# Attention outputs on one core: the values are read where they were projected, and the copy made for each head is given up

## What is computed

```python
q = x @ Wq
kv = x @ Wkv
k, v = jnp.split(kv, 2, axis=-1)
q, k, v = (to_heads(q), to_heads(k), to_heads(v))
sim = jnp.einsum('bid,bjd->bij', q, k) * scale
sim = sim + _cope(q, sim, pos_emb)
attn = jax.nn.softmax(sim, axis=-1)
out = jnp.einsum('bij,bjd->bid', attn, v)
```

## Time and profile before

| | |
|---|---|
| median of 3 runs | 2291.75 us (2290.97 to 2293.32) |
| the profiled execution's own time | 2291.38 us |
| its span, first to last instruction | 2289.5 us |
| mean granted TensorE clock | 0.993 of full speed |
| busy: TensorE, its weight loads, VectorE, ScalarE, GpSimd | 97%, 63%, 71%, 77%, 17% of the span |

### The profile page before, as it was taken

How to read it: one execution, slowest core, us unless ns; L and a number is a source line. 1 busy time by engine, 2 the same in 40 slices (tenths; PEclk the granted TensorE clock), 3 DMA queues, 4 the chain that set the end, 5 groups by cost and what they waited for, 6 DMA issues and landing times. The chain is left out here.

```text
span 2289.5 us, 53196 instructions
## 1 busy us (share of the span) xinstructions
PE 2226.8 (97%) x14577; PEld 1446.7 (63%) x14577; DVE 1633.4 (71%) x4269; ACT 1762.5 (77%) x3723; POOL 389.3 (17%) x673
## 2 busy tenths in 40 slices
PE   7999999999999999999999999999999879999997
PEld 5666666666666666666666666666665547777775
DVE  5888888888888888888888888888888811223232
ACT  5888888888888888888888888888888843455453
POOL 1111111111111111111111111111111101121121
PEclk9999999999999999999999999999999989999998
DMA  2010101010101010101010101010101021010100
GB/s 74 24 40 25 39 24 40 23 39 23 39 25 41 23 40 24 40 23 40 23 39 23 39 23 39 23 40 23 33 14 57 15 67 35 30 39 30 39 30 7
DMA packets 109392, 75.44 MB, mean 33 GB/s; under 512 B 28077, under 2 KB 105070, under 8 KB 109294
## 3 DMA queue, kind: packets, MB, share of 16 engines
q1 hardware_dynamic: 109294, 73.95, 11.6%
HBM read 14.33 MB, written 2.10 MB: 7 GB/s over the span
## 5 line engine op out<-in xcount | busy, mean ns | idle before, releaser
L842 DVE TENSOR_REDUCE mx<-Sc 128x1 f32<-128x1024 f32 (+1 forms) x512 | 568.0, 1130 | 245.1 <-PE Sc L632 244.8
L483 ACT ACTIVATE probsT<-rings 128x512 f32<-128x512 f32 x1024 | 554.1, 594 | 194.6 <-PE rings L640 194.4
L640 PEld LDWEIGHTS rings<-ident,probs 128*128 128x128 f32 x4096 | 437.0, 141 | 304.4 <-issue 103.1
L507 ACT ACTIVATE probs<-Sc,nbias 128x1024 f32<-128x1024 f32 x512 | 566.9, 1112 | 27.9 <-DVE nbias L852 27.9
L640 PE MATMUL rings<-ident,probs 128*128 128x128 f32 x4096 | 566.6, 281 | 3.0 <-ACT probs L507 2.5
L632 PE MATMUL Sc<-qk,q_now 64*128 64x512 f32 x2048 | 531.3, 616 | 10.5 <-ACT probs L507 9.1
L654 PE MATMUL out<-probsT,V_now 128*64 128x256 f32 x4096 | 498.3, 385 | 0.0
L805 DVE COPY_PREDICATED z<-mask,z 128x224 f32<-128x224 int16 (+5 forms) x768 | 393.3, 512 | 11.1
L375 POOL TENSOR_TENSOR prod<-cut,z 128x350 f32<-128x350 f32 x128 | 120.7, 943 | 1466.8 <-DVE z L817 1466.8
L654 PEld LDWEIGHTS out<-probsT,V_now 128*64 128x64 f32 x4096 | 271.4, 136 | 153.6 <-issue 42.5
L632 PEld LDWEIGHTS Sc<-qk,q_now 64*128 64x128 f32 x2048 | 177.5, 186 | 115.9 <-issue 100.6
(11 more groups left out here) (128 smaller groups left out, 2256.8 us busy)
## 6 DMA issues: line engine op xcount, KB each, us to landing
q_now<-qk SPq DMA_DIRECT2D x256, 64.0 KB, 2.0
xv<-xT SPq DMA_DIRECT2D x113, 128.0 KB, 2.2
q_far<-qk SPq DMA_DIRECT2D x256, 32.0 KB, 1.8
V_now<-V SPq DMA_DIRECT2D x16, 512.0 KB, 3.0
at<-attn SPq DMA_DIRECT2D x16, 512.0 KB, 3.2
probs<-in_x_dram SPq DMA_DIRECT2D x4, 512.0 KB, 5.5
wqk<-in_L_attn_Wq_dram SPq DMA_DIRECT2D x32, 64.0 KB, 2.1
xin<-in_x_dram SPq DMA_DIRECT2D x16, 128.0 KB, 2.8
```

The lines of the kernel that those rows point to most:

```text
L483: nc.scalar.activation(probsT[:, u, 4 * s:4 * s + 4, :], ring[k % 2][:, :].rearrange("p (t q) -> p t q", q=P), ACT.Copy).then_inc(slot_out, 1)
L507: nc.scalar.activation(probs[:, u, cols], Sc[:, cols], ACT.Exp, bias=nbias[:, u:u + 1], accum_out=sums[:, u, half:half + 1]).then_inc(exp_ ...
L640: last = nc.tensor.transpose(ring[k % 2][:, j * P:(j + 1) * P], probs[:, u, (4 * s + j) * P:(4 * s + j + 1) * P], ident[:, :])
L842: nc.vector.tensor_reduce(mx[:, u, half:half + 1], Sc[:, cols], AX.X, ALU.max).then_inc(dve_unit, 1)
```

## The change

The tile `V_now`, the semaphore `v_in`, the function `load_values` and all its 16 DMAs are taken out. `outputs` gets an argument `keys`, the head whose values it needs, and reads slot `keys % 4` of `V`. Since `outputs(g - 1, ...)` is issued in step `g`, the first step of a head passes the head before. The heads are written out one by one in TensorE's program, so `keys` is a plain number everywhere and the addresses are fixed ones.

```diff
-        V_now = sb("V_now", [P, NT, C])
...
-        v_in = sem("v_in")
...
-            def load_values(g):
-
-                sp.dma_start(V_now[:, :, :], V[:, (g // PAIRS) % 4, :, :]).then_inc(v_in, 16)
-
             sp.wait_ge(slot_out, 8 + 2 * PAIRS)
-            load_values(0)
...
                 load_now(g + 1, not odd)
-                if head:
-
-                    wait_apart(sp, out_full, g, waited)
-                    load_values(g)
                 if tile:
...
-            def outputs(g, base, slots, tiles, empty=True):
+            def outputs(g, base, slots, tiles, keys, empty=True):
 
                 if tiles[0] == 0:
                     if empty:
                         pe.wait_ge(halves_out, g)
-                    wait_apart(pe, v_in, g // PAIRS * 16 + 16, waited)
                 for t in tiles:
                     if t % 4 == 0:
                         pe.wait_ge(slot_out, base + slots[t // 4] + 1)
                     half = t % 2 * C
-                    last = nc.tensor.matmul(out[half:half + C, 0:2 * P], V_now[:, token_tile(t), :],
+                    last = nc.tensor.matmul(out[half:half + C, 0:2 * P], V[:, keys % 4, token_tile(t), :],
                                             probsT[:, :, t, :], start=t < 2, stop=t >= NT - 2)
...
             def head(at, par, start=0, **kw):
 
+                keys = at // PAIRS
                 if start == 0:
-                    body(at, False, par, new_keys=True, **kw)
-                    body(at + 1, True, par, **kw)
+                    body(at, False, par, new_keys=True, keys=keys - 1, **kw)
+                    body(at + 1, True, par, keys=keys, **kw)
```

More of the change, by code:

```diff
@@ L286, in _, with body @@
             weights(1)
-            def load_values(g):
-                sp.dma_start(V_now[:, :, :], V[:, (g // PAIRS) % 4, :, :]).then_inc(v_in, 16)
             sp.wait_ge(slot_out, 8 + 2 * PAIRS)
-            load_values(0)
-            def body(g, odd, late=False, first=False, tile=True, far=True, head=False, near=False):
+            def body(g, odd, late=False, first=False, tile=True, far=True, near=False):
                 base = slots_before(g, late)
@@ L323, in _ @@
             with sp.Fori(1, LASTV // PAIRS - 1) as h:
-                body(h * PAIRS, False, head=True)
+                body(h * PAIRS, False)
                 body(h * PAIRS + 1, True, near=True)
@@ L330, in _ @@
                 weights(h + 2)
-            body(LASTV - PAIRS, False, head=True)
+            body(LASTV - PAIRS, False)
             body(LASTV - PAIRS + 1, True, near=True)
@@ L336, in _ @@
             weights(H - 1, values=False)
-            body(LASTV, False, tile=False, head=True)
+            body(LASTV, False, tile=False)
             body(LASTV + 1, True, tile=False, near=True)
@@ L343, in _ @@
             load_early(sp, A, A["ctx_in"])
-            body(LASTP, False, late=True, tile=False, head=True)
+            body(LASTP, False, late=True, tile=False)
             body(LASTP + 1, True, late=True, tile=False)
@@ L667, in body @@
             def body(g, odd, par, late=False, first=False, proj=True, val=True, far=True, far_par=None,
-                     second=False, new_keys=False):
+                     second=False, new_keys=False, keys=0):
                 base = slots_before(g, late)
@@ L690, in body @@
                     transposes(1, base, at.last, 3)
-                    outputs(g - 1, base, at.last, range(EARLY_TILES), empty=not second)
+                    outputs(g - 1, base, at.last, range(EARLY_TILES), keys, empty=not second)
                 if far:
@@ L703, in body @@
                 if not first:
-                    outputs(g - 1, base, at.last, range(EARLY_TILES, NT))
+                    outputs(g - 1, base, at.last, range(EARLY_TILES, NT), keys)
                 if proj:
@@ L711, in head @@
             def head(at, par, start=0, **kw):
+                keys = at // PAIRS
                 if start == 0:
-                    body(at, False, par, new_keys=True, **kw)
-                    body(at + 1, True, par, **kw)
+                    body(at, False, par, new_keys=True, keys=keys - 1, **kw)
+                    body(at + 1, True, par, keys=keys, **kw)
                 with pe.Fori(2, PAIRS - 2, 2) as t:
-                    body(at + t, False, par, **kw)
-                    body(at + t + 1, True, par, **kw)
+                    body(at + t, False, par, keys=keys, **kw)
+                    body(at + t + 1, True, par, keys=keys, **kw)
                 if "late" in kw:
                     return
-                body(at + PAIRS - 2, False, par, far_par=1 - par, **kw)
-                body(at + PAIRS - 1, True, par, far_par=1 - par, **kw)
+                body(at + PAIRS - 2, False, par, far_par=1 - par, keys=keys, **kw)
+                body(at + PAIRS - 1, True, par, far_par=1 - par, keys=keys, **kw)
             body(0, False, 0, first=True)
@@ L730, in _ @@
             head(LASTP, 1, late=True, proj=False, val=False)
-            body(G - 2, False, 1, late=True, proj=False, val=False, far=False)
-            body(G - 1, True, 1, late=True, proj=False, val=False, far=False)
+            body(G - 2, False, 1, keys=H - 1, late=True, proj=False, val=False, far=False)
+            body(G - 1, True, 1, keys=H - 1, late=True, proj=False, val=False, far=False)
             base, at = slots_before(G, True), Slots()
@@ L741, in _ @@
             transposes(1, base, at.last, 3)
-            outputs(G - 1, base, at.last, range(NT))
+            outputs(G - 1, base, at.last, range(NT), H - 1)
             pe.wait_ge(scaled, 2 * (G - 1))
```

## The result

The changed kernel takes 2297.3 us (median of 10 executions, 2296.35 to 2301.3), the kernel before 2292.53 us (10 executions, 2290.66 to 2295.89). The ratio is 1.0024, 95% interval [1.0015, 1.0034]: 4.8 us slower, just over the 0.2% that the prediction called no change. The forecast was 2291.4 us and no change. The profiled execution of the changed kernel took 2296.35 us, with a span of 2294.3 us.

What follows compares the result with a forecast made beforehand. TensorE's own matmul stream was taken to bound the kernel. Terms 0 (wait) + 0 (tile) + 0 (15 copies) - 0.4 us (first copy) gave 2291.4 us, called no change, range 2288.5 to 2294.0 us.

Steps and rivals of the forecast that it cites:

- The wait ahead of the output matmuls, 128 times: TensorE's wait for copied values before each step's first output matmuls; removing it was put at 0 us.
- The tile: Output matmuls load weights from `V` instead of `V_now`; claimed cost 0, with 17 ns per load hidden.
- The fourth rival: Weight loads from `V` in all output matmuls take longer; slower, up to 147 us, 2439 us; chance 0.06.
- The 15 copies: Copies to `V_now` inside the loop, at each later head's first step; removing them was put at 0 us gain.
- The first copy: Copy ahead of the loop, issued before the `q_far` loads; removing it was to gain 0.4 us.
- The wait for `q_far`: TensorE's idle time in step 0; forecast to fall from 3.28 to about 1.8 us.
- the 0.17 us of the maxima: Step 0, tile 1: waiting inside VectorE's two maxima, 2.34 against 2.17 us, which could go.
- the 0.32 us: Step 0, tile 1: delay from finished bias to exponential, while ScalarE copies late transposes; could go.
- The clock rival: At the start, shorter idle time keeps TensorE's clock up; -2.7 us, 2289.0 us; chance 0.12.
- VectorE's 1.00: VectorE's busy share in a microsecond of the start, cited against more of the earlier `q_far` coming through.
- The pause of 0.17 us: Before each output run's first weight load; forecast to stay; a rival had 21.8 us come back, 2270 us, chance 0.04.
- the row of the second run: Each step's second output run has no wait for values, yet pauses 0.17 us; taken as proof of 0 gain.

Runs made afterwards that it cites:

- read_v: Kernel before with one edit: the outputs read `V`, copies to `V_now` still issued and waited for; ratio 0.9995.
- apart_halves: Changed kernel with the `halves_out` wait in its own instruction where the `v_in` wait stood, in step 1 a long-met wait; ratio 1.0 against the kernel before.
- again: The changed kernel run again without any edit; ratio 1.0018 against the kernel before, 2295.5 us.
- two_q_before: Kernel before with two tiles for `q_now`, loaded a step earlier; ratio 0.9993 against the kernel before, 2291.2 us.

## Why the prediction was wrong

**What bounds the kernel.** Right that the matmul stream bounds it, and that no DMA is waited for in the trace of before. What I did not work out is the margin: "no wait" was a landing at 2.0 us for a need at 2.4 to 2.8 us, on DMA engines that also carry 84 loads of 16 KB of code.

**The step that failed** is "The wait ahead of the output matmuls, 128 times": "Its cost on the path is 0", with "the remaining wait for `halves_out` stays where it was, so nothing is added". As an instruction it does cost 0: pauses of 39.1 against 39.4 us, no idle time before the outputs, a head of 113.50 us. But the edit changed TensorE's stream, and with it how often its instruction loads fall where they make `q_now` late (the first placing in seven of eight traces with the stream as before and in none of eight with a changed one; the 63rd load at 103.08). That the instructions run at no cost was taken for "the edit costs nothing". The same gap is in the rivals: the order of instructions was given as proof that "nothing else moved". The measured price is 2.4 us of waits for `q_now` in the trace of the change; by the medians the kernel is 4.8 us slower, of which a second tile for `q_now` takes away some 3 to 4 us.

**The tile**: right, 0 (`read_v` 0.9995; loads of 132 to 138 ns). The fourth rival, slower by weight loads, had the sign of the result and a wrong mechanism. **The 15 copies**: right within the interval (`apart_halves` 1.0), though a cost of up to about 2 us for taking them out is not excluded. **The first copy**: right. The wait for `q_far` fell from 3.28 us to 2.04 us, not to 1.8 us, with 0.52 us for the exponential behind it; the 0.17 us of the maxima and nearly all of the 0.32 us came back as forecast. From the first scores of step 0 to those of step 2 the change takes 25.91 us, the kernel before 26.37 us: 0.46 us for a forecast of 0.4 us. **The clock rival** did not happen in the trace of the change: the granted clock in that place was again 0.50, from 40 to 42 us. In `again` it stayed at 1.00 from 40 to 43 us, and the same stretch took 25.91 us too, so a higher clock gives nothing there, as VectorE's 1.00 had said. What I missed is the other side: in the two traces with the copy in which the clock stayed at 1.00 (`read_v`, 2nd, and `two_q_before`), the stretch takes 25.90 us with the copy in place. In these traces the 0.4 us are a gain only where the clock falls. **The pause of 0.17 us** stayed (39.1 us in 235 pauses against 39.4 us in 236), as the row of the second run had said. By the rule that the prediction took from the Trainium skill, page "TensorE: Matmul & The Clock Gate", section "The mechanism", up to 21.8 us would have come back; this trace does not bear that out.

**What stays open.** The traced waits for `q_now` are 1.3 to 3.2 us in the kernels with a changed stream. What the rest of the 4.8 us is was not separated: the stretch behind the loop scatters by 4.7 us, in part with short falls of the granted clock, which come and go in traces of either kernel, and the missing copies may cost up to some 2 us. Why the number and the form of the wait together decide how often the second placing occurs was not found.

## What to carry to other kernels

A load that lands 0.4 to 0.8 us ahead of its use is not safely hidden: before calling an edit free, work out the margin of each transfer that the bounding engine needs in every round, and ask what could delay it by 2 us. In a kernel that is written out at length, an edit of one instruction can move the loads of the program onto such a transfer, so a change of 0.2% may come from the placement alone; put the removed instruction back as an empty one, or trace one program several times, before giving the change a cause. Split the difference of two spans by stretches as well: more than half of this one lay outside the loop. A second tile that lets the load go a step earlier takes the sensitivity away.

## What the runs showed of the hardware

Packets of 16 KB on the instruction queue, which I take for TensorE's program, occupy one DMA engine for 0.9 to 1.7 us (eighteen traces). They delay data on that engine: a 64 KB transfer in 16 parts, one of which met such a packet, landed 3.1 to 4.2 us after its issue instead of 2.0 us, in 16 of 18 cases 1.0 to 1.1 us after the packet's end, and at step 103 of the change the other 31 of 32 semaphore updates were on time. I had not expected that the same program places these loads in two ways, from execution to execution (`read_v`: third load at 2.71 or at 3.12). The execution with the second placing took 2297.83 us, the others 2291.24 and 2289.58 us, of which the waits for `q_now` are 3.2 us.
